# Loading order, bank places and work of the first input in a fused attention and feed-forward kernel

## The reference, cut to what matters

```python
def _dynamic_conv(x, w_kgen, b_kgen, w_conv, b_conv):
    context = x.mean(axis=1)
    gate = jax.nn.sigmoid(context @ w_kgen.T + b_kgen).mean(axis=1)
    y = depthwise_conv3(x, w_conv) + b_conv          # over tokens, kernel size 3
    return y * gate
...
h = _dynamic_conv(x, ...)
q, k, v = h @ w_q.T, h @ w_k.T, h @ w_v.T            # 16, 4 and 4 heads of 64
w = softmax(q @ kc * scale, axis=-1)                 # per chunk of 64 keys
out = (w @ vc * w.sum()).sum(chunks) / (w.sum().sum(chunks) + 1e-9)
x = _layernorm(x + out @ w_o.T)
for l in range(2):                                   # the layers
    q, k = rotary(l2norm(q) * q_scale), rotary(l2norm(k) * k_scale)
    x = x + local_attention(q, k, v) @ wo
    x = x + (a * gelu(g)) @ w2 + b2                  # a, g = ln(shift(x)) @ w1 + b1
```

## Time and profile before

| | |
|---|---|
| median of 3 runs | 1357.25 us (1355.5 to 1358.14) |
| the profiled execution | 1355.71 us, span 1353.2 us |
| mean granted TensorE clock | 0.984 of full |
| PE busy | 1216.0 us (90%), 12352 matmuls |
| DVE busy | 1125.9 us (83%), 2210 instructions |
| POOL busy | 1068.6 us (79%), 1431 instructions |
| ACT busy | 953.8 us (70%), 1772 instructions |
| DMA | 44.28 MB, 12.4% of 16 engines' span |

### The profile page before, as it was taken

The page is one execution under the profiler, slowest core; times in us unless marked ns, Lnnn a source line. Parts: engine busy times, 40 slices in busy tenths (PEclk is TensorE's granted clock), DMA queues, the critical chain, the costliest instruction groups (busy, mean ns, idle before and its releaser), DMA issues.

```text
span 1353.2 us, 37200 instructions
## 1 busy us (share of the span) xinstructions
PE 1216.0 (90%) x12352; PEld 985.1 (73%) x12352; DVE 1125.9 (83%) x2210; ACT 953.8 (70%) x1772; POOL 1068.6 (79%) x1431
## 2 busy tenths in 40 slices
PE   3899999999999999986789999999999999999985
PEld 2577777777777778775567777777777777777764
DVE  2788898898889888894888888888888898989873
ACT  3466766766766676664668888888888787878762
POOL 0876676666666666668899999999999999999971
PEclk9799999999999999998999999999999999999998
DMA  5000000000000000000211111211212212121110
GB/s 179 4 11 13 10 9 12 12 12 12 12 12 10 12 12 8 9 12 8 50 41 44 49 42 42 52 40 43 51 46 51 51 42 52 42 51 44 47 39 24
DMA packets 87053, 44.28 MB, mean 33 GB/s; under 512 B 43908, under 2 KB 80048, under 8 KB 86960
## 3 DMA queue, kind: packets, MB, share of 16 engines
q1 hardware_dynamic: 86960, 43.08, 12.4%
HBM read 19.99 MB, written 6.29 MB: 19 GB/s over the span
## 4 chain that ended last, share of the span: by engine, by line
POOL 28%; PE 26%; issue 19%; DVE 17%; ACT 6%; SPq 2%; DVEq 1%; ACTq 1%; POOLq 1%; DMA 0%
POOL rnorm L716 9%; POOL kT L705 7%; DVE probs L1100 6%; PE bank L1397 4%; POOL probs L766 4%; DVE mx L1091 3%; POOL kT L719 3%; PE bank L1426 2%; PE bank L1533 2%; PE bank L1359 2%; PE bank L1494 2%; PE bank L1512 2%; PE bank L1568 2%; DVE sums L1083 2%; SPq L473 2%
## 5 line engine op out<-in xcount | busy, mean ns | idle before, releaser
L655 POOL TENSOR_TENSOR probs<-probs,coef 128x1024 f32<-128x1024 f32 x128 | 240.9, 1904 | 5.0
L716 POOL TENSOR_TENSOR rnorm<-norm,halves 128x8 f32<-128x8 f32 x128 | 213.7, 1669 | 10.7
L1091 DVE TENSOR_REDUCE mx<-bank 128x8 f32<-128x512 f32 x256 | 164.2, 683 | 34.8 <-PE bank L1397 34.4
L849 ACT ACTIVATE probs<-probs 128x1024 f32<-128x1024 f32 x128 | 135.5, 1058 | 54.2 <-DVE probs L1100 54.1
L1083 DVE TENSOR_REDUCE sums<-probs 128x16 f32<-128x1024 f32 x128 | 154.2, 1213 | 22.4 <-ACT probs L849 22.4
L705 POOL TENSOR_TENSOR kT<-qT 128x512 f32<-128x512 f32 x128 | 163.6, 1278 | 6.9 <-DVE qT L1177 6.9
L1100 DVE TENSOR_TENSOR probs<-bank,mx 128x512 f32<-128x512 f32 x256 | 161.2, 672 | 0.0
L719 POOL TENSOR_TENSOR kT<-kT,rnorm 128x512 f32<-128x512 f32 x128 | 133.4, 1042 | 10.0
L1382 PE MATMUL bank<-ident,probs 128*128 128x128 f32 x1024 | 137.0, 277 | 4.8 <-ACT wT L843 4.8
L843 ACT ACTIVATE wT<-bank 128x512 f32<-128x512 f32 x256 | 138.0, 596 | 1.2 <-PE bank L1382 1.2
L857 ACT ACTIVATE oT<-bank 128x256 f32<-128x256 f32 x128 | 47.9, 374 | 125.8 <-PE bank L1415 125.8
(11 more groups left out here) (130 smaller groups left out, 3107.2 us busy)
## 6 DMA issues: line engine op xcount, KB each, us to landing
probs<-f_v SPq DMA_DIRECT2D x96, 128.0 KB, 2.3
res<-stage_x SPq DMA_DIRECT2D x48, 128.0 KB, 3.7
xn<-in_x SPq DMA_DIRECT2D x16, 128.0 KB, 2.2
xr<-in_x SPq DMA_DIRECT2D x16, 128.0 KB, 2.1
stage_x<-xo SPq DMA_DIRECT2D x32, 64.0 KB, 1.6
hn<-stage_x SPq DMA_DIRECT2D x32, 64.0 KB
mn<-mid SPq DMA_DIRECT2D x64, 32.0 KB
stage_x<-yo SPq DMA_DIRECT2D x16, 128.0 KB, 2.1
```

Source lines behind the costliest of these rows:

```text
L655: nc.gpsimd.tensor_tensor(out=e[:, :, :, :], in0=e[:, :, :, :], in1=coef[r % 2][:, 2, A_REP * at:A_REP * (at + 1), :].unsqueeze(3).broadca ...
L716: nc.gpsimd.tensor_tensor(out=rnorm[:, at], in0=norm2[:, 1, at], in1=halves[:, 0:F_HEADS], op=ALU.pow).then_inc(rnorm_set, 1)
L849: nc.scalar.activation(e[:, :, :, :], e[:, :, :, :], ACT.Exp).then_inc(exp_done, 1)
L1091: nc.vector.tensor_reduce(mx[s % 2][:, 2 * k:2 * k + 2, :], banks[2 * (s % 2) + k][:, :].rearrange("p (h c k) -> p h c k", h=2, c=CHUNKS), ...
```

## The change

What it does, by engine:

- SP loads in the order: input 0, identity (a semaphore of its own, `ident_in`), the four other small tables (`gate_weights_in`), wk and wq (`qk_weights_in`), input 1, wv and wo (`a_weights_in`), `xr` 0 and 1. In the body of turn 0 it loads inputs 2 and 3, and then the 44 transfers for the layers.
- ACT runs one exponential on a single column before it waits for anything but the constants, copies input 0 without waiting for the small tables, and leaves the outer taps of input 0 out.
- DVE adds the outer taps of input 0 with two `scalar_tensor_tensor`. In turn 0 it does `gate_weights(1)` after the first step's subtraction and `gate_logit(1)` after the second's.
- PE starts when input 0 and the identity are there, projects in the order k 0, q 0, q 1, k 1 into banks 4, 5, 6 and 7, transposes input 1 into bank 4, and in turn 0 computes the first two steps' scores ahead of the fills, with the wait for wv and wo behind them.
- POOL leaves the convolution of input 0 out, builds the rotary tables in step pairs 4 and 5 of turn 0 (two multiplications in each), where it waits for `weights_in`, and splits the layers' weights in turn 1, one part in each of its first six step pairs.

```diff
-            return (self.pre.index((kind, local)) + len(self.pre)) % 2
+            return self.pre_places[self.pre.index((kind, local))]
...
-    pre = [("xT", 0), ("gate", 0), ("q", 0), ("q", 1), ("k", 0), ("k", 1), ("xT", 1)]
+    pre = [("xT", 0), ("gate", 0), ("k", 0), ("q", 0), ("q", 1), ("k", 1), ("xT", 1)]
...
+    return SharedBanks(order, pre, stride, ("o", "out"), pre_places=[0, 1, -2, -1, 0, 1, -2])
...
             def pre():
                 load(xn[0], 0, xn_in[0])
+                sp.dma_start(ident[:, :], t["eye"]).then_inc(ident_in, 16)
...
+                for dst, src in ((wk[:, :, :, :].rearrange("p k a d -> p (k a d)"), t["wkT"]), (wq[:, :], t["wqT"])):
+                    sp.dma_start(dst, src).then_inc(qk_weights_in, 16)
+                load(xn[1], 1, xn_in[1])
+                for dst, src in ((wv[:, :], t["wvT"]), (wo[:, :, :], t["woT"].rearrange("(m p) n -> p m n", p=P))):
                     sp.dma_start(dst, src).then_inc(a_weights_in, 16)
-                load(xn[1], 1, xn_in[1])
                 load(xr[0], 0, xr_in[0])
                 load(xr[1], 1, xr_in[1])
+
+            def layers_weights():
...
                         load(xn[p], b + 2, xn_in[p])
+                    if turn == "first" and p == PAIR - 1:
+                        layers_weights()
...
             def convolution(b):
 
-                pool.wait_ge(taps_set, b + 1)
+                pool.wait_ge(taps_set, b)
...
+                    if turn == "first" and s >= A_STEPS // 2:
+                        if s == A_STEPS // 2:
+                            pool.wait_ge(weights_in, 16 * N_WEIGHTS)
+                        if s < A_STEPS // 2 + A_GROUP * LAYERS:
+                            rotary_tables_scaled((s - A_STEPS // 2) // A_GROUP)
+                    if isinstance(i, int) and i == 1 and s < A_GROUP * 3 * LAYERS:
+                        split_weights(*divmod(s // A_GROUP, 3))
                     for at in range(A_GROUP):
-                        if turn == "first" and s + at < 3 * LAYERS:
-                            split_weights(*divmod(s + at, 3))
...
-            stage_a(pool, a_body, a_pre)
+            stage_a(pool, a_body, lambda: gate_denominator(0))
...
             def pre():
                 act.wait_ge(consts_set, N_CONSTS)
+                nc.scalar.activation(rstd[0][:, 0:1], minus[:, 0:1], ACT.Exp)
+                x_transposed(0, 0, "pre", 0)
                 act.wait_ge(gate_weights_in, 16 * N_GATE_WEIGHTS)
-                x_transposed(0, 0, "pre", 0)
                 middle_tap(0)
-                outer_taps(0)
                 gate_exponential(0)
                 gated_input(0)
...
                 gate_weights(0)
+                dve.wait_ge(tap_set, 1)
+                nc.vector.scalar_tensor_tensor(conv[:, 1, :], xT[:, 0:SEQ], wconv[:, 0:1], conv[:, 0, :],
+                                               ALU.mult, ALU.add).then_inc(conv_set, 1)
                 gate_logit(0, 0, "pre")
+                dve.wait_ge(conv_set, 1)
+                nc.vector.scalar_tensor_tensor(conv[:, 2, :], xT[:, 2:SEQ + 2], wconv[:, 2:3], conv[:, 1, :],
+                                               ALU.mult, ALU.add).then_inc(conv_set, 1)
                 gated(0)
-                gate_weights(1)
...
+                    starts = turn == "first" and s == 0
-                    if quarter == 0 and prepares(turn, p):
+                    if quarter == 0 and prepares(turn, p) and not starts:
                         gate_logit(PAIR * i + p + 1, p + 1, turn)
...
+                    if starts:
+                        gate_weights(1)
                     if exists(turn, s):
                         maximum(n + 1, s + 1)
                         subtracted(n + 1, s + 1)
+                    if starts:
+                        gate_logit(1, 1, turn)
...
             def pre():
-                pe.wait_ge(gate_weights_in, 16 * N_GATE_WEIGHTS)
+                pe.wait_ge(ident_in, 16)
...
-                pe.wait_ge(a_weights_in, 16 * N_A_WEIGHTS)
+                pe.wait_ge(qk_weights_in, 16 * N_QK_WEIGHTS)
...
+                    if turn == "first" and s == 0:
+                        scores(i, s)
+                        scores(i, s + 1)
+                        pe.wait_ge(a_weights_in, 16 * N_A_WEIGHTS)
                     if exists(turn, s, PV_LAG):
                         weights_turned(n - PV_LAG, late)
                     fill(s, p, main)
...
-                    if exists(turn, s):
+                    if exists(turn, s) and not (turn == "first" and s == 0):
                         scores(i, s)
                         scores(i, s + 1)
```

More of the change, by code:

```diff
@@ L75, with __init__ @@
     BEFORE = {"drain2": "drain", "drain": "last", "last": "middle", "middle": "middle", "second": "first", "first": "pre"}
-    def __init__(self, order, pre, stride, late, places=None):
-        self.order, self.pre, self.stride, self.late = order, pre, stride, late
+    def __init__(self, order, pre, stride, late, places=None, pre_places=None):
+        self.order, self.pre, self.stride, self.late, self.pre_places = order, pre, stride, late, pre_places
         self.places = places or [at % 2 for at in range(len(order))]
@@ L96, in before @@
         if turn == "pre":
-            at = self.pre.index((kind, local)) - 2
-            return (*self.pre[at], 0) if at >= 0 else None
+            at = self.pre.index((kind, local))
+            same = [f for f in self.pre[:at] if self.bank(*f, "pre") == self.pre_places[at]]
+            return (*same[-1], 0) if same else None
         own = self.order.index((kind, local))
@@ L121, in stage_a_banks @@
         order += [("o", s - PV_LAG), ("o", s + 1 - PV_LAG)]
-    pre = [("xT", 0), ("gate", 0), ("q", 0), ("q", 1), ("k", 0), ("k", 1), ("xT", 1)]
+    pre = [("xT", 0), ("gate", 0), ("k", 0), ("q", 0), ("q", 1), ("k", 1), ("xT", 1)]
     stride = {"xT": PAIR, "gate": PAIR, "k": 2 * PAIR, "q": 4 * PAIR, "v": PAIR, "o": A_STEPS, "out": A_SLOTS}
-    return SharedBanks(order, pre, stride, ("o", "out"))
+    return SharedBanks(order, pre, stride, ("o", "out"), pre_places=[0, 1, -2, -1, 0, 1, -2])
 A_FILLS = {
@@ L294, in build @@
         zrstd = [sb(f"zrstd{p}", [P, 2, TILES]) for p in range(PAIR)]
-        gate_weights_in, a_weights_in, weights_in = sem("gate_weights_in"), sem("a_weights_in"), sem("weights_in")
+        ident_in, gate_weights_in, qk_weights_in, a_weights_in, weights_in = (
+            sem(n) for n in ("ident_in", "gate_weights_in", "qk_weights_in", "a_weights_in", "weights_in"))
         consts_set = sem("consts_set")
@@ L303, in build @@
         read = {k: sem(f"{k}_read") for k in A_BANKS.stride}
-        wk_ctx_set, gate_exp, gate_plus, gate_step, taps_set, conv_set, shift_set, hT_set = (
-            sem(n) for n in ("wk_ctx_set", "gate_exp", "gate_plus", "gate_step", "taps_set", "conv_set", "shift_set", "hT_set"))
+        wk_ctx_set, gate_exp, gate_plus, gate_step, tap_set, taps_set, conv_set, shift_set, hT_set = (
+            sem(n) for n in ("wk_ctx_set", "gate_exp", "gate_plus", "gate_step", "tap_set", "taps_set", "conv_set", "shift_set", "hT_set"))
         scored, max_set, sub_done, exp_done, sum_done, inverse_set, share_step, total_set, coef_set, normed = (
@@ L337, in build @@
         SHARE_STEPS = 4
-        N_GATE_WEIGHTS, N_A_WEIGHTS, N_WEIGHTS = 5, 4, 2 + LAYERS * (6 + 3 * F_CHUNKS + 6)
+        N_GATE_WEIGHTS, N_QK_WEIGHTS, N_A_WEIGHTS, N_WEIGHTS = 4, 2, 2, 2 + LAYERS * (6 + 3 * F_CHUNKS + 6)
         N_CONSTS, N_F_CONSTS, N_PADS = 11, 6, 4
@@ L682, in a_body, with rotary_tables_scaled @@
                         normalise_chunks(A_STEPS // A_GROUP * i + s // A_GROUP, s // A_GROUP)
+                    if turn == "first" and s >= A_STEPS // 2:
[5 more added lines that the diff above has]
+                        split_weights(*divmod(s // A_GROUP, 3))
                     for at in range(A_GROUP):
-                        if turn == "first" and s + at < 3 * LAYERS:
-                            split_weights(*divmod(s + at, 3))
                         if beside:
                             beside(s + at)
[L689 to L696, removed]
-            stage_a(pool, a_body, a_pre)
+            def rotary_tables_scaled(l):
+                for tile in range(TILES):
+                    nc.gpsimd.tensor_tensor(out=table[l][:, tile, :, :], in0=rotary[:, tile, :, :], in1=qk_scale[l][:, :, :],
+                                            op=ALU.mult).then_inc(tables_set, 1)
+            stage_a(pool, a_body, lambda: gate_denominator(0))
             def layers_program():
@@ L786, in x_transposed @@
                 act.wait_ge(made["xT"], b + 1)
-                wait(act, taps_set, b)
+                wait(act, taps_set, b - 1)
+                if local == 1 and turn == "pre":
+                    act.wait_ge(conv_set, 2)
                 wait(act, wk_ctx_set, b)
@@ L794, in middle_tap @@
                 act.wait_ge(read["xT"], b + 1)
```

(4 more changed lines are left out.)

8 lines of the change are left out of this document (2 added, 6 removed).

## The result

The changed kernel takes 1343.6 us (median of 5, 1342.59 to 1349.37) against 1357.25 before; the ratio is 0.9908, 95% interval 0.9885 to 0.9931. It is faster by some 0.9%, 13.65 us by the medians where 11.4 were forecast. The profiled executions, 1355.71 before and 1342.59 after, differ by 13.1, their spans by 12.5.

A forecast was written before the change was run, and what follows sets the result against it. Stage A was taken as a full machine keeping any earlier start, with losses at its beginning. Gains 10.1 + 2.0 - 0.7 = 11.4 us from 1355.71 give 1344.3; the median stands 1.5 higher, 1345.8, stated range 1342 to 1351.

The forecast's parts named there:

- The start: Before the first maxima: the chain to hT gains 3.45 us; first maxima at 16.4 instead of 22.56, 6.2 earlier.
- The hole: First to second step pair: transpose of input 2 stops waiting for its load; gains 10.1 us, 12.0 at full clock.
- the case chosen: First to second maxima: TensorE stays at the slow clock, second maxima at 29.65, a gain of 10.1 us.
- The next four pairs: Step pairs behind the second maxima, without POOL's splits there: 2.0 us gained, between 1.0 and 3.2.
- Turn 1: One split in each of six pairs: 0.7 us lost through late shares in two pairs, bounds 0 and 2.6.
- Carried to the end: Stage A onward: an earlier start is kept to the end; the layers' stage starts 10 to 13 us earlier.
- the likeliest case: The whole-kernel forecast itself: hole, pairs and turn 1 together, range 1343.5 to 1349 us, 69 in 100.
- POOL binds: Rival in turn 1: each split costs 1.0 us in six pairs; loss 6 instead of 0.7, 1351 us, 10 in 100.
- The rival of no change: Splits and tables in their new place cost what was gained, 11.4 + 2.8 us: 1355 to 1357, 3 in 100.
- The rival of a slower kernel: TensorE at half speed over three full pairs: 24 us lost against 11.4 gained, 1370 us, 4 in 100.
- The clock stayed high: Rival: second pair starts at 27.75 and thin pairs run at full clock; 14.5 us gained, 1342.8, 14 in 100.

The follow-up runs named there:

- e8_old_head: Changed kernel with input 0's start undone: PE waits for all small tables, no early exponential, convolution on ACT and POOL; 1346.91 us.
- c_after2: The changed kernel itself, unaltered, run again for comparison on the same chip; 1343.55 us, ratio 0.9896 to the kernel before.
- e4_no_preload: Changed kernel without ACT's early exponential, so its table load comes with the copy of input 0; 1344.33 us, median of three.
- e7_two_splits: Changed kernel with two weight splits in each of turn 1's first three step pairs instead of one in each of six; 1351.29 us.
- e1_loads_old: Changed kernel with the layers' 44 transfers issued ahead of the loads of inputs 2 and 3 again; 1355.19 us.
- e2_pool_old: Changed kernel with POOL's rotary tables back ahead of turn 0 and the splits back in its first three pairs; 1363.26 us.

## Why the prediction was right, and where its sizes were off

**The start: right.** PE at 3.29 (3.2), `wk_ctx` 5.91 (5.83), logit 6.95 (7.0), `hT` 8.46 (8.6), first scores 15.07 (15.2), first maxima 16.25 (16.4). The additions of two SBUF operands took 0.48 each, the 0.47 of the nearest row. By `e8_old_head` the chain's part is 3.7. The early exponential, which the text counted as done in time and gave no price, is worth 0.1. One correction stays: the 2.1 us by which the scores pass the fills are real at the first maxima and 0.3 at the second.

**The hole: right in mechanism, 0.9 too small.** 10.1 was the sum, 10.99 the measurement. ACT's queue came out in the order given, each link a little shorter: the copy of input 2 at 24.16, and PE, where the text had 25.5, at 24.66. The clock was the lower one, as the case chosen had it: 2.08 for the projection, 3.79 for the scores.

**The next four pairs: the term most off, and the one that moves.** 2.0 was forecast between 1.0 and 3.2; it was 3.58 (38.06 to 34.48), above the upper bound, which its own terms put at 3.3 (1.03 + 0.6 + 1.7). In `c_after2` the same four pairs took 36.00, a gain of 2.06, nearly the forecast. The difference of 1.5 between two profiles of one program is luck, not mechanism. `e4_no_preload` divides it: there the same four pairs, free of splits but at clocks of 0.86 and 0.73 in the first two, took 36.89. So about 1.2 us belong to the splits, 1.02 of them in the pair where DVE had waited 1.03 for POOL, and 2.4 to the clock. By pair the gain was 0.59, 1.81, 0.16 and 1.02; the first two are the 0.6 and 1.7 that the text gave for full clock and counted by about half. They came in full, though the first pair had a clock of 0.91.

**Turn 1: 0.41 for 0.7, by a miscount.** DVE waited 0.29 for POOL in the one quarter 0 that has a split ahead of it. The text counted two; the other quarter 0 of the turn comes before the first split. The other five splits cost nothing, as reasoned. Nor do the tables: they stand at 69.13 and 78.45, in windows of 9.31 and 8.94 us, which took 9.31 and 8.93 in the kernel before.

**Carried to the end: nearly.** 14.57 at the fifth window, 14.03 at the last maxima, 12.5 in the span. The last difference was not forecast. Profiles of the changed kernel, unaltered, had 747.5 to 749.2 in that stretch, so one profile doesn't show a cost there.

**The sum and the range.** By the first profile hole, pairs and turn 1 gave 10.99 + 3.58 - 0.41 = 14.16 where the sum had 11.4, so each term erred to the same side. The range of the likeliest case does not follow from its terms: they run from 8.5 (10.1 + 1.0 - 2.6) to 15.2 (12.0 + 3.2), that is from 1342 to 1349, not from 1343.5. The measured 1343.6 lies inside both, in the stated one by 0.1.

**Rivals.** That POOL binds did not happen with one split a pair, and did with two. The rival of no change had splits and tables cost their full time; they cost 0.4. Its own sum, 14.2 against 12.1 gained, would also have been 2 us slower, about 1359, and not 1355 to 1357. The rival of a slower kernel had the lower clock over full pairs; all of them ran at 1.00, and 0.86 or 0.87 was seen over full pairs only in `e7_two_splits`. The kernels that did come out unchanged or slower, `e1_loads_old` and `e2_pool_old`, did so by other mechanisms. The clock stayed high in the thin pairs of the first profile (0.91 and 1.00), but not in the hole. The page TensorE: Matmul & The Clock Gate of the Trainium skill (HAM oscillation) had bursts with long waits between them cold; this case agrees at 4.55 us of wait (2.08 for the projection) and shows the other side at 1.86 (1.13). The length of the wait alone does not settle it: in the changed kernel a key projection took 1.13 after 2.96, and the output products of the drain took 2.02 or 3.40 after the same 1.82.

## What to carry to other kernels

A load's place in a queue and the work that waits for another load in that queue are one change: with one half or the other undone, the whole change was worth 2 us or minus 6, with both in place 13.65. After moving something off the path, read the bracket of the same instruction again; here the wait went from DMA to ACT, and reordering ACT's queue at that place gave another 2.8 and 3.8 us. Idle time of an engine takes extra work in small pieces spread over many steps: one split a pair cost 0.4 us in all, two a pair cost 6.0 more in the same turn and 9.0 more in the time.

## What the runs showed of the hardware

The same pair of the same program took 8.81 us at a granted TensorE clock of 0.91 and 10.32 at 0.83. The pair behind it took 7.80 at 1.00 and 9.44 at 0.73 in `e4_no_preload`, whose program differs by one instruction at the very start, though DVE (7.64 in both) and not PE is the busiest engine there. The three profiles of the changed kernel differ by this much at single places while its three medians agree within 1.4 us, so a difference of 1 to 2 us in one such window is not yet a cause. These places are few: from the sixth step pair of stage A on, each pair has the same length within 0.1 us in all 14 kept profiles, except for the pairs of turn 1 that splits delay and the one in the drain of `e7_two_splits`.

A wait of 1.5 to 2.2 us on DVE cost a full step pair 3.2 and 2.8, with PE's clock at 0.86 and 0.87 over the pair in place of 1.00. A like wait of PE, 1.82 in the drain, was followed by the full clock in one profile and the lower one in another, so no run here shows what decides it.
